# Summing the two scan directions in TensorE, a merge that loads half of the results, and single-slot multiplies in the scan

## The reference

```
xc     = silu(conv(x @ W_in));   z = silu gate
delta  = softplus(W_dt @ dts + bias)          # dts, B, C = W_x @ xc, per token
h_t    = exp(delta_t * A) * h_(t-1) + (delta_t * u_t) * B_t      # 16 states per channel
y_t    = sum over states of (h_t * C_t)  + D * u_t
```

## Time and profile before

| what | value |
|---|---|
| median of 3 runs | 35480.57 us (35474.87 to 35480.98) |
| the profiled execution | 35494.41 us, its span 35492.3 us |
| VectorE busy | 92% of the span |
| GpSimd busy | 87% |
| TensorE busy | 72%, mean granted clock 0.837 of 2.4 GHz |
| ScalarE busy | 54% |

### The profile page before, as it was taken

How to read it: one execution, slowest core, us unless ns; L and a number is a source line. 1 busy time by engine, 2 the same in 40 slices (tenths; PEclk the granted TensorE clock), 3 DMA queues, 4 the chain that set the end, 5 groups by cost and what they waited for, 6 DMA issues and landing times. The chain is left out here.

```text
span 35492.3 us, 317452 instructions
## 1 busy us (share of the span) xinstructions
PE 25552.7 (72%) x72136; PEld 7774.6 (22%) x72136; DVE 32715.3 (92%) x14737; ACT 19066.4 (54%) x23309; POOL 30722.6 (87%) x7768
## 2 busy tenths in 40 slices
PE   6777777777766777777777766777777777766776
PEld 2222222222222222222222222222222222222222
DVE  6999999999976999999999986999999999985995
ACT  5555555555534555555555534555555555544553
POOL 1999999999961999999999961999999999972996
PEclk8888888888888888888888888888888888887888
DMA  5666666666674666666666664666666666675666
GB/s 170 175 176 175 176 176 176 176 176 177 176 217 155 177 177 177 176 177 177 177 177 176 176 208 164 174 176 176 176 176 177 176 177 177 176 207 178 176 177 187
DMA packets 2407103, 6321.11 MB, mean 178 GB/s; under 512 B 701776, under 2 KB 873680, under 8 KB 2395856
## 3 DMA queue, kind: packets, MB, share of 16 engines
q1 hardware_dynamic: 2405328, 6305.89, 67.0%
HBM read 2904.96 MB, written 764.47 MB: 103 GB/s over the span
## 5 line engine op out<-in xcount | busy, mean ns | idle before, releaser
L1291 POOL TENSOR_TENSOR h<-h,c 128x2048 f32<-128x2048 f32 x4992 | 20766.6, 4180 | 261.9 <-DVE h L1091 165.8
L1091 DVE TENSOR_TENSOR_SCAN h<-decay,state,slots 128x1024 f32<-128x1024 f32 x6240 | 14307.0, 2336 | 126.3 <-ACT state L1235 12.4
L996 PE MATMUL psy<-h,t_fold 128*32 128x512 f32 x40000 | 10436.1, 672 | 4.6 <-POOL h L1291 4.6
L1130 ACT ACTIVATE decay<-delta,na 128x1024 f32<-128x1024 f32 x6248 | 7127.0, 1149 | 2985.8 <-DVE h L1091 2673.9
L1087 DVE TENSOR_TENSOR_SCAN h<-slots,state,made 128x1024 f32<-128x1024 f32 x3744 | 8554.2, 2328 | 132.1 <-ACT slots L1130 131.0
L1312 POOL TENSOR_TENSOR made<-du,b 128x2048 f32<-128x2048 f32 x1872 | 7821.6, 4178 | 676.8 <-DMA b<-bcdram 676.8
L919 PE MATMUL slots<-bc,pick 96*128 96x512 bf16 x6248 | 2328.0, 461 | 7926.1 <-DVE h L1087 6871.9
L1064 DVE TENSOR_TENSOR slots<-du,slots 128x2048 f32<-128x2048 f32 x3120 | 7165.4, 2297 | 700.8 <-PE slots L919 298.6
L1130 ACT ACTIVATE slots<-delta,na 128x1024 f32<-128x1024 f32 x3744 | 4173.5, 1116 | 4990.3 <-DVE h L1091 4988.7
L996 PEld LDWEIGHTS psy<-h,t_fold 128*32 128x32 f32 x40000 | 2201.8, 120 | 7758.5 <-issue 7507.4
L1304 POOL TENSOR_TENSOR du<-delta,u 128x1024 f32<-128x1024 f32 x628 | 1477.0, 2352 | 2260.1 <-ACT delta L1184 2260.1
(11 more groups left out here) (119 smaller groups left out, 19140.2 us busy)
## 6 DMA issues: line engine op xcount, KB each, us to landing
delta<-delta SPq DMA_DIRECT2D x10048, 128.0 KB, 2.6
du<-du SPq DMA_DIRECT2D x10048, 128.0 KB, 3.0
b<-bcdram SPq DMA_DIRECT2D x7520, 128.0 KB, 2.8
c<-bcdram SPq DMA_DIRECT2D x6720, 128.0 KB, 2.9
u<-useq SPq DMA_DIRECT2D x212, 1536.0 KB, 6.9
yseq<-ybuf SPq DMA_DIRECT2D x624, 512.0 KB, 2.9
useq<-ready SPq DMA_DIRECT2D x84, 2048.0 KB, 6.6
ya<-yseq SPq DMA_DIRECT2D x288, 512.0 KB, 4.9
```

Of the source, the lines that this page charges most:

```text
L996: mm = pe.matmul(psy[rows, cols], T["fold"][:, :], h[v % H_RING][:, c, cols], start=(v % QUADS == 0), stop=(v % QUADS == QUADS - 1), skip_ ...
L1091: dve.tensor_tensor_scan(out, decay[s % DECAY_RING][:, order], slot[s % 2][:, order], first, ALU.mult, ALU.add).then_inc(sem["h_ready"], 1)
L1130: act.activation(dst, delta4[j % DELTA_RING][:, s % 2, :], ACT.Exp, scale=na[q][:, k:k + 1])\
L1291: pool.tensor_tensor(both[:, :, 0:CH], both[:, :, 1:], c4[g][:, order].unsqueeze(1).broadcast_to((P, 2, CH)), ALU.mult)\
```

## The change

Five things are done.

1. *One product per slot.* The PSUM tensor `slots` becomes two tensors `slot0` and `slot1`. TensorE fills both (two bf16 matmuls of 512 columns each instead of two for both), and VectorE multiplies each by itself, 1,024 elements at a time, without waiting for the scans before.
2. *y of both directions in one array.* In the first half of a sequence's bodies each direction stores its y. In the second half, where a direction comes to a chunk that the other one has done, SP loads the stored y into `ybuf` (`load_y`), TensorE adds it into `psy` through the identity, and the sum is stored to the same place. `yseq` is half as large. The two loops of the scan on SP and TensorE are written as a first and a second half.
3. *Rows in place.* In `psy` the two column halves of y lie on partitions 0-63 and 64-127, and the pair of groups picks the bank. The four fold matmuls of a unit thus write four groups of 32 partitions in one bank, where they wrote two groups in two banks. The skip term D*u becomes four matmuls of 64 output rows. Store and load of y are two DMAs each.
4. *The merge loads one array.* Row jobs are loaded straight into `total`; only column jobs go through `ya` and a VectorE addition. `yb`, the row additions and `pair_up` are gone.
5. *Another order.* `load_b` goes ahead of `load_c` in SP's queue; the second half of a tile's delta is spread at unit 6 instead of 4; projection, sums and the B and C chain move by a few steps. Both fills of a unit are issued at the odd step of the unit before.

```diff
-DELTA_AT = (0, 1)
+DELTA_AT = (1, 1)
-SUM_AT = (4, 4, 5, 5, 6, 6, 7, 7)
+SUM_AT = (3, 3, 5, 5, 5, 5, 7, 7)
-XDBL_AT = [(0, 10), (0, 10), (0, 11), (0, 12), (0, 13), (0, 14)]
+XDBL_AT = [(0, 11), (0, 11), (0, 11), (0, 13), (0, 13), (0, 13)]
-DELTA_OUT_AT, DU_OUT_AT = (3, 4), (4, 7)
+DELTA_OUT_AT, DU_OUT_AT = (3, 6), (4, 7)
...
+                def load_y(i, C0, T_):
+                    sp.wait_ge(sem["y_stored"], C0 * (32 * TILES) + 32 * (T_ + 2))
...
+                        sp.dma_start(ybuf[2 * GROUP * a:2 * GROUP * a + 2 * GROUP, :].rearrange("p (r f) -> p r f", r=2),
+                                     halves[HALVES - 1 - a if backward(q) else a]).then_inc(sem["y_back"], 16)
...
+                    if new_b:
+                        load_b(on_pool.index(v) + B_RING)
                     if new_c:
                         load_c(v + QUADS)
-                    if new_b:
-                        load_b(on_pool.index(v) + B_RING)
...
-                        mm = pe.matmul(slot[0][:, cols], pick[:, rows_of, :], bc[q % 2][:, cols],
+                        mm = pe.matmul(slot[s % 2][:, cols], pick[:, rows_of, :], bc[q % 2][:, cols],
...
+                        pe.wait_ge(sem["y_back"], backs * (32 * BODY_TILES) + 32 * (v // TILE_UNITS + 1))
                         for cols in HALF:
+                            pe.matmul(psy[:, cols], T["ident"][:, :], ybuf[:, cols][:, order], start=False, stop=False,
...
+                    bank = HALF[pair_of(v) % 2]
+                    for a, cols in enumerate(HALF):
                         for c in range(2):
-                            rows = slice(first + GROUP * c, first + GROUP * c + GROUP)
-                            mm = pe.matmul(psy[rows, cols], T["fold"][:, :], h[v % H_RING][:, c, cols],
+                            rows = slice(2 * GROUP * a + GROUP * c, 2 * GROUP * a + GROUP * c + GROUP)
+                            mm = pe.matmul(psy[rows, bank], T["fold"][:, :], h[v % H_RING][:, c, cols],
...
-                    dve.wait_ge(sem["h_ready"], C0 * STEPS + (2 * v + H_START))
...
-                    dve.tensor_tensor(slots[:, ::-1, :], du4[j % DU_RING][:, ::-1, 1:],
-                                      slots[:, 0:1, :].broadcast_to((P, 2, CH)), ALU.mult)\
-                        .then_inc(sem["b_multiplied"], 2)
+                    dve.tensor_tensor(slot[s % 2][:], du4[j % DU_RING][:, s % 2, 1:], slot[s % 2][:], ALU.mult)\
+                        .then_inc(sem["b_multiplied"], 1)
...
+                    if w == "row":
+                        signal = y_in[to][c] if last else row_in[to][t]
+                        sp.dma_start(total[to][:, t, c * CH:(c + 1) * CH], y_v[0, pair, c, t]).then_inc(signal, 16)
                         return
...
-                    pool.tensor_tensor(ya[s][:], ya[s][:], yb[s][:], ALU.add).then_inc(sem["paired"], 1)
```

More of the change, by code:

```diff
@@ L881, in _, with body @@
                     after_gate(0, 0, v)
-                with sp.Fori(0, NC // BODY_CHUNKS) as i:
+                def body(i, second):
                     C0 = i * BODY_CHUNKS
@@ L885, in _ @@
                         after_gate(i, C0, v)
+                        if second and v < BU and v % TILE_UNITS == Y_BACK:
+                            load_y(i, C0, v // TILE_UNITS)
                         if v < BU:
                             chunk_work(i, C0, v)
-                sp.wait_ge(sem["y_stored"], 16 * (NC * TILES + 2))
+                if both_ways:
+                    with sp.Fori(0, G) as g:
+                        for second in range(2):
+                            with sp.Fori(0, NCH // 2) as e:
+                                body(g * NCH + second * (NCH // 2) + e, second)
+                else:
+                    with sp.Fori(0, NC // BODY_CHUNKS) as i:
+                        body(i, 0)
+                sp.wait_ge(sem["y_stored"], 32 * (NC * TILES + 2))
                 sp.wait_ge(sem["x_full"], 80 * (NC + 1))
@@ L1047, in _ @@
                         if s % 2 == 1:
-                            reduce(C0, s // 2 - REDUCE_LAG)
+                            reduce(C0, s // 2 - REDUCE_LAG, backs)
+                if both_ways:
+                    with pe.Fori(0, G) as g:
+                        for second in range(2):
+                            with pe.Fori(0, NCH // 2) as e:
+                                body(g * NCH + second * (NCH // 2) + e, g * (NCH // 2) + e if second else None)
+                else:
+                    with pe.Fori(0, NC // BODY_CHUNKS) as i:
+                        body(i, None)
                 for v in range(REDUCE_LAG):
@@ L1345, in merge_stage @@
     JOBS = len(jobs)
-    ops, loads, per_slot = [], [], [0] * DEPTH
-    for j, (w, t, c) in enumerate(jobs):
-        ops.append((ops[-1] if ops else 0) + (2 if w == "col" and kind == "snake" else 1))
-        per_slot[j % DEPTH] += 2 if K > 1 else 1
-        loads.append(per_slot[j % DEPTH])
+    cols = [j for j, (w, t, c) in enumerate(jobs) if w == "col"]
+    ops = [sum(2 if kind == "snake" else 1 for k in cols if k <= j) for j in range(JOBS)]
     OPS = ops[-1]
-    COLS = sum(w == "col" for w, t, c in jobs)
-    def cols_to(j):
-        return sum(w == "col" for w, t, c in jobs[:j + 1])
-    assert JOBS % DEPTH == 0
+    LOADS = len(cols) // DEPTH
     jobs_at = [range(JOBS * c // NB, JOBS * (c + 1) // NB) for c in range(NB)]
@@ L1367, in merge_stage @@
         block_in = [sem["block_in0"], sem["block_in1"]]
+        row_in = [[sem[f"row_in{j}{t}"] for t in range(TILES)] for j in range(2)]
         gate_in = [sem["gate_in0"], sem["gate_in1"]]
@@ L1372, in merge_stage @@
         ya = [] if last else [sb(f"ya{j}", [P, CH]) for j in range(DEPTH)]
-        yb = [] if last else [sb(f"yb{j}", [P, CH]) for j in range(DEPTH)]
         total = [sb(f"total{j}", [P, TILES, L]) for j in range(2)]
@@ L1719, in _ @@
             def _(pool):
-                def pair_up(count, j):
-                    if jobs[j][0] == "row":
-                        return
-                    s = j % DEPTH
-                    pool.wait_ge(job_in[s], count * (16 * per_slot[s]) + 16 * loads[j])
-                    pool.tensor_tensor(ya[s][:], ya[s][:], yb[s][:], ALU.add).then_inc(sem["paired"], 1)
                 pool.sem_inc(sem["gated"], 2)
-                for j in range(JOBS):
-                    pair_up(0, j)
                 for i in range(PAIRS // 2):
```

164 lines of the change are left out of this document (82 added, 82 removed).

## The result

| | before | after |
|---|---|---|
| median, us (runs) | 35,480.98 (5) | 35,325.75 (5) |
| lowest to highest, us | 35,474.87 to 35,497.76 | 35,308.80 to 35,419.07 |
| profiled span, us | 35,492.3 | 35,324.0 |
| granted clock, mean | 0.837 | 0.801 |
| the four scans, first to last `made`, us | 30,565.8 | 30,650.1 |

The ratio is 0.996 (0.9945 to 0.9974). The time lies in the stated range, but the change is a quarter of the forecast one. A scan is taken here from the start of GpSimd's first product `made` of a layer to the start of its last, a merge from there to the start of the last gate product; both come from the trace rows of these two tiles. The merges gave 83.1 + 103.5 + 78.0 = 265 us of the 310 forecast. The scans gave nothing of the other 310: they lost 84.

What follows compares the result with a forecast made beforehand. VectorE was taken to bound the kernel, by 2.6 us to a chunk over GpSimd. Scans 310 us plus merges 310 made 620 us, giving 34,874 us from the profiled span or 34,860 from the median; range 34,430 to 35,380.

Steps and rivals of the forecast that it cites:

- two terms of 310 us: The scans were to give 310 us (1.5 to each of 208 chunks) and the three merges together another 310.
- Title step, the multiply and its second fill: In the scan: narrow multiplies shorten a unit by 0.28 us, the second fill costs 0.1; 2.7 us to a chunk gained.
- TensorE's other work ... cost nothing: In unit 7: skip, stored y and fold, 5.1 us with the fill, hide in a unit of 6.8; no cost.
- The projection of delta: At a tile's start: queued behind the second fill, it makes ScalarE's decays late; 1.2 us to a chunk lost.
- B first: In the scan: loading B earlier removes GpSimd's wait of 2.8 us to a chunk; given nothing in the sum.
- The merge: Fewer loads and additions: 48 us from the opening, 55 from three pairs; 103 us per merge, 310 for three.
- A: In the scan: the fills go well and GpSimd's work sets the chunk; 34,460 us, chance 0.16.
- B: The scan gives nothing: multiplies do not overlap or delta's lateness eats the gain; 35,170 us, chance 0.17.
- C: At a tile's start: TensorE at 1.2 GHz loses 6.6 us to a chunk; 36,540 us, chance 0.13.

Runs made afterwards that it cites:

- 11: The kernel before with only B loaded ahead of C and the second store of delta at step 6: 35,342 us, 0.9964.
- 2: The changed kernel with the one wide multiply per unit and the single fill of the kernel before: 35,114 us, 0.9895.
- Experiments 2 to 4: The changed kernel with wide multiply and single fill (35,114 us), then the stored y left out of the changed kernel (35,073) and of that wide form (35,083).
- 6: The changed kernel with the sums of step 5 of the tile moved to step 4: 35,476 us, 1.0001.
- 9: The changed kernel with skip product and stored y behind unit 6's fold, and delta's projection at step 0 ahead of the fills: 35,523 us, 1.0011.
- Experiment 7: The changed kernel with skip product and stored y moved from unit 7 to behind unit 6's fold, y loaded one unit earlier: 36,196 us, 1.0204.
- 12: The kernel before with B loaded ahead of C in SyncE's queue and nothing else: 35,349 us, 0.9963.
- 10: The changed kernel with one fill per unit and two multiplies of 1,024, from slot 0 into slot 1, then in place: 35,108 us, 0.9893.

## Why the prediction was wrong

Of the sum's two terms of 310 us the merges gave 265 and the scans -84. That the time still lies in the stated range is owed to the width of the range and not to the mechanism.

The four scans together, by one trace of each kernel, give the account:

| step | scans, us | difference |
|---|---|---|
| before | 30,565.8 | |
| B first and the later store (11) | 30,407.4 | -158 |
| stored y, skip, fold and the tables, wide form (2) | 30,448.6 | +41 |
| narrow multiplies with two fills (the changed kernel) | 30,650.1 | +201 |

**Title step, the multiply and its second fill: failed.** The form was right (6.74 us, 0.11 late at the low clock) and was to give 2.7 us to a chunk, 562 us. It cost 201. I priced what the second fill does to its own multiply, and not what it does to everything behind it in TensorE's queue.

**"TensorE's other work ... cost nothing": this is the step that failed.** It set 5.1 us of work against a unit of 6.8 and gave the unit's whole length as cover. But the second fill starts only once VectorE has begun the unit, and the next pair must be filled when it ends. In the changed kernel's rows, the block from 5073.44 to 5080.39 has to fit between the fill's end and the end of the scans at 5079.26, 5.8 us, and the next fill takes 0.65 of these: 5.2, not 6.8. The block was forecast as 1.7 + 1.7 + 1.1 = 4.5; it is 4.9 at the high clock (1.94, 1.98 and 1.06, with overlaps) and 7.0 here. Experiments 2 to 4 show it: the stored y costs 31 us where one fill is asked for and 253 where two are. So do the tiles of the changed kernel, 2000 to 9000 us: of the 72 with the stored y, 16 had the block at 5.0 us or less and none of them a late fill; of the 56 at 5.5 or more 49 had one, 62.8 us together, and the 72 tiles without the stored y had none. The sums of step 5, a second such block (experiments 6 and 9; 43.1 us in unit 4), weren't in the sum at all. Nor was the wait of unit 7 for decays, behind the next chunk's projection: 52.0 us in the changed kernel, 11.8 in that of 2. What makes it longer with two fills was not tried.

**The projection of delta: the mechanism was right, the size depends on the state of TensorE.** Both of its cases occurred, 1.98 us behind a full queue and 3.78 behind a wait, and the low one cost 1.87 us to a tile where 2.2 was worked out. (That sum was itself off: 5.1 + 2.2 + 1.12 is 8.4 against 6.74, so the first decay would be 1.7 late and not 1.2; it was 1.40.) In the changed kernel unit 2 has 20.7 us of such waits in 7000, 0.4 to a chunk against the 1.2 taken. Experiment 7 put every tile in the low case. What I missed is that the two terms hang together: the block that makes a fill late in unit 1 also keeps TensorE busy until the projection. Removing the one wait makes the other.

**B first: failed in size.** "I give it nothing in the sum" was wrong by 136 us. A wait of the engine with 2.6 us of slack did reach VectorE. The link that the traces support: GpSimd's gate products come late, with them the folds in TensorE's queue, the loads that SyncE issues behind a gate, and the next chunk's projection, which needs these loads. TensorE's wait for its loads ahead of that projection was 75.3 us before, 9.8 in the run of 11 and 8.0 in that of 12. ScalarE's wait for that projection fell from 274.8 us before to 167.4 in the run of 11, and with it VectorE's waits in unit 7, which were 38, 48.6 us together. No run took a single link out, so the order of the links is argued.

**The merge: right, 265 for 310.** The opening gave 46 for 48, layer 0's three pairs 38 for 55; pairs of 142.8 and 143.2 us with the gate's load awaited, for 135, are where it fell short.

**Rivals.** A, GpSimd as the bound, didn't come: it still waits 157.6 us for VectorE. B, that the scan gives nothing, came nearest in its time, 35,170, but not in its reason: multiplies did overlap, and only a few late fills and decays took it back. C, the low clock, is half true, but its 36,540 us didn't come. Granted fell from 0.837 to 0.801, yet at 0.79 the wide form has no such waits. The low clock costs where it lengthens a block that already has a deadline: the 16 blocks at the high clock made no fill late, and of the 56 slower ones 49 did. The Trainium skill, "TensorE: Matmul & The Clock Gate", Part 1, has the idle engine at 1.2 GHz; the rows of experiment 7 agree (3.78 us after a wait, 1.98 without).

**What stays open.** The waits of one kernel differ by layer (scan of layers 0, 1, 2: 9,381, 9,443 and 9,484 us in the changed kernel, 9,375, 9,366 and 9,370 in that of 2); which coincidences make the third longer was not tried. Nor was a third slot, which would end the second fill's wait. The best complete kernels are those of 2 and 10, 35,114 and 35,108 us, 1.1% under before.

## What to carry to other kernels

In an in-order queue, the cover of a piece of work is not the length of the period: it is the stretch from the end of the last wait ahead of it to the first deadline behind it, and each further wait shortens that for everything that stands behind. So a change that adds a wait is costed by listing all that is queued after it, here at the low clock where TensorE had just waited. And a wait on an engine with a little slack isn't free as long as other engines' queues hang on its results: a swap of two loads was worth 136 us here, half of what all three merges gave.

## What the hardware showed that I hadn't expected

- The same matmuls in the same place take twice as long after a wait of TensorE as behind a full queue: delta's projection 3.78 and 1.98 us, the skip product 3.68 and 1.94. Taking 4 us of work away from in front of the projection made the kernel 870 us slower.
- Two VectorE multiplies of 1,024 take the time of one of 2,048 (2.36 and 2.30 us). What the narrow form saves, 0.28 us to a unit, lies in the handovers: successive operations start 0.08 to 0.09 us before the one ahead has ended where no completion is waited for.
- The fold in four groups of 32 partitions of one bank takes 1.06 us for 8 records, in two groups 1.91. The Trainium skill, "TensorEngine Tiling (Array Packing)", Key Properties, lets different tiles run in parallel, and this agrees; no drain was seen between the skip product's 64-column form and the stored y behind it (5073.44 + 3.68 against 5077.05), nor between that and the fold (5077.05 + 2.35 against 5079.33); the ends of matmuls are modelled, so a short one isn't excluded.
